# VectorE's order between two attention tiles: the maximum completed first, then the row sum's inverse and the query's blocks; the spread one key tile later

## What is computed

```python
kp = k @ Wk.T;  vp = v @ Wv.T + bv;  qp = layernorm(x) @ Wq.T + bq     # k = v = context rows, 3202 x 512
probs = softmax(qp @ kp.T / sqrt(512))                                  # 4096 x 3202
x = x + (probs @ vp) @ Wo.T + bo
g = softmax(layernorm(x) @ w_router)                                    # 16 experts
# each token goes to its two best experts, at most 512 tokens per expert
y[token] = sum over its two experts of p * (silu(xe @ w_gate) * (xe @ w_fc)) @ w_proj
out = x + y
```

## Time and profile before

| | |
|---|---|
| median of three runs | 1741.78 us |
| the profiled execution | 1741.16 us |
| its span in the profile | 1739.4 us |
| mean granted clock of TensorE | 0.968 |
| TensorE busy | 1606.2 us (92%) |
| VectorE busy | 1164.9 us (67%) |
| GpSimd busy | 873.4 us (50%) |
| ScalarE busy | 719.1 us (41%) |

### The profile page before, as it was taken

One profiled execution on the slowest core, in us unless ns is written; L12 is line 12 of the kernel. 1 busy time (PEld: TensorE's weight loads), 2 busy tenths in 40 slices (PEclk: granted clock), 3 DMA queues, 4 the chain that ended last, 5 costly groups with the idle time before them and its releaser, 6 DMA issues. The chain is left out here.

```text
span 1739.4 us, 41578 instructions
## 1 busy us (share of the span) xinstructions
PE 1606.2 (92%) x15821; PEld 1062.4 (61%) x15821; DVE 1164.9 (67%) x2271; ACT 719.1 (41%) x1060; POOL 873.4 (50%) x832
## 2 busy tenths in 40 slices
PE   8999989999999999999999999999997389999964
PEld 4444768666776677766777667766674144545530
DVE  4443276788777887778877888778786365555524
ACT  2443244444444444444444444444443134545440
POOL 0100064566555665566655666556665346565540
PEclk9999999999999999999999999999998689999985
DMA  4310111122111221212111121111210069899869
GB/s 157 92 43 13 50 32 44 44 47 49 44 45 43 48 48 44 51 38 56 46 44 45 44 51 45 44 45 44 50 38 25 26 196 207 216 209 215 187 96 377
DMA packets 202315, 140.93 MB, mean 81 GB/s; under 512 B 135010, under 2 KB 151394, under 8 KB 202148
## 3 DMA queue, kind: packets, MB, share of 16 engines
q1 hardware_dynamic: 179696, 94.27, 19.7%
q0 software_dynamic: 16896, 35.42, 10.6%
q10 hardware_dynamic: 5556, 8.66, 1.3%
HBM read 86.65 MB, written 51.68 MB: 80 GB/s over the span
## 5 line engine op out<-in xcount | busy, mean ns | idle before, releaser
L47 PE MATMUL sc<-qt,kT 128*128 128x128 f16 x3100 | 523.1, 219 | 12.7 <-issue 12.7
L45 PE MATMUL sc<-qt,kT 128*128 128x128 f16 x3100 | 523.1, 219 | 10.3 <-DMA qt<-blocks_q 6.7
L46 PE MATMUL sc<-qt,kT 128*128 128x128 f16 x3100 | 523.0, 219 | 0.0
L45 PEld LDWEIGHTS sc<-qt,kT 128*128 128x128 f16 x3100 | 303.2, 98 | 19.0 <-issue 13.1
L47 PEld LDWEIGHTS sc<-qt,kT 128*128 128x128 f16 x3100 | 303.2, 98 | 14.9 <-issue 14.9
L45 PE MATMUL acc<-vv,pT 128*128 128x512 f16 x800 | 305.0, 381 | 4.4 <-DVE pT L1047 4.4
L46 PE MATMUL acc<-vv,pT 128*128 128x512 f16 x800 | 305.2, 381 | 0.0
L47 PE MATMUL acc<-vv,pT 128*128 128x512 f16 x800 | 305.0, 381 | 0.0
L46 PEld LDWEIGHTS sc<-qt,kT 128*128 128x128 f16 x3100 | 303.3, 98 | 2.0
L856 POOL TENSOR_TENSOR sum<-sum,s_T 128x512 f32<-128x512 f32 (+1 forms) x160 | 281.6, 1760 | 26.4 <-ACT s_T L907 5.9
L896 ACT ACTIVATE s_T<-sc 128x512 f32<-128x512 f32 (+1 forms) x224 | 120.0, 548 | 301.4 <-PE sc L47 297.6
(11 more groups left out here) (296 smaller groups left out, 2916.5 us busy)
## 6 DMA issues: line engine op xcount, KB each, us to landing
xq<-in_x_dram SPq DMA_DIRECT2D x32, 256.0 KB, 2.7
x_in<-in_x_dram SPq DMA_DIRECT2D x32, 256.0 KB, 3.2
raw_g<-in_L_ffn_w_gate_dram SPq DMA_DIRECT2D x16, 512.0 KB
raw_f<-in_L_ffn_w_fc_dram SPq DMA_DIRECT2D x16, 512.0 KB
raw_p<-in_L_ffn_w_proj_dram SPq DMA_DIRECT2D x16, 512.0 KB
y_dram<-x SPq DMA_DIRECT2D x32, 256.0 KB, 2.0
rows_dram<-row SPq DMA_DIRECT2D x32, 256.0 KB, 2.0
y_sb<-y_dram SPq DMA_DIRECT2D x16, 512.0 KB, 16.0
```

What stands on the lines that cost most here:

```text
L45: pe.matmul(out, s_hi, m_hi, start=first, stop=False)
L46: pe.matmul(out, s_hi, m_lo, start=False, stop=False)
L47: return pe.matmul(out, s_lo, m_hi, start=False, stop=last)
```

## The change

`shift` loses its first part, the two halvings, which become `complete`, and the call of `query_blocks`. In a step VectorE now does `complete(t + 1)`, `inverse(t)`, `query_blocks(t + 2)` and `shift(t + 1)`, where it did `inverse(t)` and `shift(t + 1)` with the halvings at its start and the query's blocks inside it, behind `s_tail`. The steps written out ahead of the loop follow the same order. In `times_values` the spread stands after key tile 11 instead of 10.

```diff
-                def shift(t, h, more_q):
+                def complete(t):
 
                     dve.drain()
                     dve.tensor_tensor(rm[:, 0:2, :], rm[:, 0:2, :], rm[:, 2:4, :], ALU.max)
                     dve.drain()
                     dve.tensor_tensor(rm1[:], rm[:, 0, :], rm[:, 1, :], ALU.max).then_inc(rm_rdy, 1)
+
+                def shift(t, h):
+
                     dve.wait_ge(mx_pe, t + 1)
                     dve.reduce_max(mx[:], ps_x[:, 0:P + TAIL], AX_X)
                     dve.drain()
                     dve.tensor_scalar(diag[:], ident[:], mx[:], None, ALU.mult).then_inc(dg_rdy, 1)
                     wait_for(dve, pt_rdy, t)
                     dve.tensor_scalar(s_tail[:], ps_x[:, P:P + TAIL], mx[:], None, ALU.subtract).then_inc(st_rdy, 1)
-                    if more_q:
-                        query_blocks(t + 1)
                     dve.wait_ge(mb_pe, t + 1)
...
+                    if more:
+                        complete(t + 1)
                     inverse(t)
+                    if more_q:
+                        query_blocks(t + 2)
                     if more:
-                        shift(t + 1, 1 - h, more_q)
+                        shift(t + 1, 1 - h)
...
-                shift(0, 0, False)
+                complete(0)
+                shift(0, 0)
                 for c in range(NCH):
                     maximum(1, 1, c)
...
+                complete(1)
                 inverse(0)
-                shift(1, 1, True)
+                query_blocks(2)
+                shift(1, 1)
...
-                        if more and k == 10:
+                        if more and k == 11:
                             spread(t + 1)
```

## The result

The changed kernel takes 1721.51 us, the median of four runs (1718.67 to 1723.67), against 1741.65 us before. The ratio is 0.9892, with a 95% interval of 0.9879 to 0.9905: 1.1% faster. The forecast was 1715 us in a range of 1709 to 1726. The profiled execution took 1721.97 us, its span is 1720.2 against 1739.4: 19.2 us less. The forecast had 25.8.

The account below looks back on a forecast made before the run. The prediction took TensorE to bound the attention; 17.5 us from the late spread plus 8.3 from the query's blocks, other parts at nothing, made 25.8 off the profiled 1741.16, so 1715 us, range 1709 to 1726.

Parts of the forecast that it names:

- TensorE sets the time: Attention stretch: TensorE busy 1052.37 of 1095.00 us, so changes on other engines count only where TensorE waits for them.
- The diagonal's end is GpSimd's, not VectorE's: VectorE's `diag` before the spread: its end hangs on GpSimd's addition L816, about 0.09 us after it, not on its start.
- The late spread, 17.5 us: Spread one key tile later: 15 waits gain 0.648 us each and 13 short steps 0.60, together 17.5 us.
- check against the row of waits: Cross-check of the spread's gain: 13.8 us of `diag` waits plus 28 x 0.16 gives 18.3 us.
- The query's blocks, 8.3 us: Query transpose 2.8 us earlier: all ten TensorE waits for `qt` at the scores go, 6.7 + 10 x 0.16 = 8.3 us.
- Rival B: At the scores, the "issue" wait after the loop's return replaces the query's wait; gain only 17.5, 1723.7 us; chance 0.10.
- the second pause: "Issue" wait inside a scores chunk after the loop's return, 12.7 us in 13 times; forecast to stay as before.
- The inverse later, nothing: VectorE's inverse behind the two halvings ends 0.88 us later; covered by slack on ScalarE and GpSimd, costed at nothing.
- C: Rival: the diagonal is slow by itself, not by GpSimd's hold; 21.5 us gained, 1719.7 us; chance 0.08.
- D: Rival: VectorE's transpose holds GpSimd, delaying L838, L816 and the diagonal; 6.4 us lost, 1739.3 us; chance 0.05.
- E: Rival: VectorE reaches the diagonal late and loses to GpSimd's L820 too; 28.3 us lost, 1761.2 us; chance 0.04.
- F: Rival: the diagonal gets in ahead of GpSimd's L816, so no step waits; 29.8 us gained, 1711.4 us; chance 0.11.

Follow-up runs that it names:

- e4: The changed kernel with the diagonal made from a copy of the identity in PSUM; 0.9870 of the kernel before, 1719.41 us.
- e10: The changed kernel with the inverse first again, then the two halvings, then the query's blocks; 0.9884 of the kernel before, 1723.65 us.
- e11: The changed kernel with the identity copy in PSUM and TensorE's loop over four steps instead of two; 0.9784 of the kernel before, 1705.19 us.
- e5: The changed kernel with TensorE's loop over four steps instead of two; 0.9833 of the kernel before, 1716.59 us.
- e6: The changed kernel with TensorE's loop turned so its return lies behind key tile 12 of the values; 1.0146 of the kernel before, 1768.89 us.
- e8: The changed kernel with the identity copy in PSUM and TensorE's loop return behind key tile 12 of the values; 0.9933 of the kernel before, 1732.55 us.

## Why the prediction was right, and where it was wrong

**TensorE sets the time.** Right. The gaps sum to 19.3 us less, the span is 19.2 us less.

**The diagonal's end is GpSimd's, not VectorE's.** Right, and shown by e4, not only by the two ends that coincided. It is what made the whole sum possible: in the long step VectorE reaches `diag` 0.3 us later and nothing happens.

**The late spread, 17.5 us.** The mechanism was right, the size 3.2 us too large: 14.3. The prediction's check against the row of waits (18.3 us) did not catch this. By its own losses a step the gaps come to 21.2, since a spread that was waited for starts 0.32 us ahead of the next product instead of 0.22, which idle time does not count. Short steps gained their 0.60 but for two. What was missing: the second step, where nothing was waited for and 0.7 us now is, since VectorE does the transpose ahead of `mx` with no slack; the first long step of the loop, 0.5 us, where GpSimd's work stands later against TensorE; two early short steps, 0.3 each; and 0.1 us in each of 13 long steps, from L816's 0.09.

**The query's blocks, 8.3 us.** This step failed. The transfer did move as computed: the write goes out 0.7 us behind the transposed maximum where it was 3.5, and in the long steps `qt` lands 1.9 to 3.5 us before TensorE is free for it. But the sum took a wait that the profile puts to one releaser for a wait that had one. "All ten waits go" was worth 2.2 us, since the instructions fetched for the return came at nearly the same moment; the idle time changed its name from "DMA qt" to "issue". Rival B named the right cause, but saw it in the second pause alone and priced it at all 8.3 us. The second pause, which the sum left as it was, shrank from 14.8 to 12.0 us. In all 13 returns of both kernels it begins behind the 35th product of the scores and ends 1.2 to 1.5 us after a second instruction packet; that packet begins 0.64 us after the first scores on average before and 0.48 after the change, and takes 1.07 and 1.03 us. Why it begins sooner was not tried.

**The inverse later, nothing.** The inverse moved as computed: ScalarE waits 167.3 us for `p_rel` where it waited 141.4, 0.8 us a step. The cost of nothing is not contradicted: e10 is the same as the changed kernel within the measurement, which leaves up to 5 us open.

**The number.** 1721.51 us is 6.5 above the forecast of 1715 and 2.2 below rival B's 1723.7; it lies inside the range because the range held B too. The terms missed by 3.2 and 6.1 us, and the 2.8 us of the second pause, which the sum had at nothing, made up a part: that is luck.

**Rivals.** C is out by e4. D and E are out: L838 took 0.99 and the transpose 1.24. F did not come: the diagonal never got in ahead of L816, which it would have to.

## What to carry to other kernels

When a wait is put down to one semaphore, ask what else ended at nearly that moment: if a loop returns there, its instructions may be next in line, and removing the named cause only renames the wait. A loop's return is cheap to make rarer (four steps in the body instead of two gave 0.6%), and costly right behind a wait. And an operation that takes four times as long in the loop as alone is better freed of what holds it than only moved: the late spread took back 14.3 of the 21.2 us, and reading one operand from PSUM took 0.96 us off it in a long step and 0.5% off the kernel (e11 against e5).

## What the runs showed of the hardware

- A product of 128 x 128 by a scalar on VectorE, f32 in SBUF, ends 0.09 to 0.10 us after the GpSimd addition L816 beside it, in 29 of 32 steps of the kernel before and of the changed one, whether its record starts 0.1 us ahead of the addition's or 0.8 behind it: 0.56 to 1.48 us long, against 0.29 with GpSimd idle and 0.35 with the matrix in PSUM and GpSimd busy. The rule in the Trainium skill ("SBUF — State Buffer", section "Who interferes with whom") that the two exclude each other for a whole instruction fits; a block transpose of 1024 f16 values did not take part in it (1.24 us, with L838's 0.99 and L820's 1.27 beside it).
- At the return of its loop TensorE starts 1.5 to 2.0 us after the end of a 16 KB instruction packet, which takes 0.9 to 1.9 us itself. The packet itself began 1.1 to 1.8 us after the semaphore of the diagonal where the return stood behind it. With twelve products or more between that semaphore and the return the pause was 0 to 1.5 us, with six 2.0 to 2.5, with three 2.6 to 3.3.
- Behind pauses of 3 us amid dense work the granted clock fell to half in e6 (eight stretches, 41 us; mean clock 0.956 against 0.967 in the changed kernel), hardly in e8 (two stretches, 7 us; 0.966) with pauses as long. What tells the two apart is open.
